# Natural scores of a transformer block: 18 units of 64-query blocks instead of 20 units of 128-query tiles, and another place for them between the expert matmuls

## What is computed

```python
xn = layernorm(x)
q, k, v = split(xn @ w_in.T + b_in)                 # 16 heads of 8
scores = einsum('bhqd,bhkd->bhqk', q / sqrt(8), k) + causal_bias
out = (softmax(scores) @ v).reshape(...) @ w_out.T + b_out
combine = top-2 of softmax(xn @ gate_w.T), normalised, * 2.5
g = silu(xn @ w_gate[e]) * (xn @ w_up[e])           # each expert
y = sum_e combine[e] * (g @ w_down[e]) + shared(xn)
return x + nan_to_zero(out) + y
```

## Time and profile before

| what | value |
|---|---|
| median of 3 runs | 585.33 us (584.45 to 585.44) |
| the profiled execution | 584.21 us |
| its span, first to last instruction | 582.5 us |
| PE, DVE busy | 91%, 81% of the span |
| ACT, POOL busy | 59%, 55% |
| natural scores, maxima on DVE (L1248) | 195.1 us in 224 instructions |
| score matmuls (L561), mask matmuls (L552) | 61.7 and 42.4 us, overlapping |

### The profile page before, as it was taken

How to read it: one execution, slowest core, us unless ns; L and a number is a source line. 1 busy time by engine, 2 the same in 40 slices (tenths; PEclk the granted TensorE clock), 3 DMA queues, 4 the chain that set the end, 5 groups by cost and what they waited for, 6 DMA issues and landing times.

```text
span 582.5 us, 13217 instructions
## 1 busy us (share of the span) xinstructions
PE 531.7 (91%) x4568; PEld 296.5 (51%) x4568; DVE 469.3 (81%) x836; ACT 342.1 (59%) x463; POOL 322.1 (55%) x345
## 2 busy tenths in 40 slices
PE   2779899989999999999999999999999999999985
PEld 1345533656336762476426663366625664366622
DVE  5989788898868978699768988689787988579704
ACT  5422497354973369534893459634794348744593
POOL 2036644675346845478354864478454782558652
PEclk9889999998999999999999999999999999999999
DMA  8994037600376006820168003750069103580001
GB/s 266 270 218 106 11 109 187 160 2 9 110 201 162 2 11 181 226 62 0 63 190 225 0 9 127 210 132 0 9 181 253 35 0 100 173 210 0 11 1 36
DMA packets 45917, 62.03 MB, mean 106 GB/s; under 512 B 4832, under 2 KB 30016, under 8 KB 45888
## 3 DMA queue, kind: packets, MB, share of 16 engines
q1 hardware_dynamic: 43180, 58.40, 36.7%
q10 hardware_dynamic: 2708, 3.24, 1.8%
HBM read 45.24 MB, written 15.34 MB: 104 GB/s over the span
## 4 chain that ended last, share of the span: by engine, by line
PE 58%; ACT 10%; DVE 8%; issue 7%; POOL 4%; POOLq 0%; DVEq 0%; ACTq 0%
PE banks L667 9%; ACT probs L928 8%; PE banks L526 7%; PE banks L561 6%; PE banks L542 6%; PE banks L528 6%; PE banks L527 6%; PE banks L640 6%; DVE neg_max L1248 3%; PE banks L543 3%; PE banks L544 3%; POOL hid_lo L1018 2%; POOL probs L1038 1%; POOL probs L1010 1%; PE banks L552 1%
## 5 line engine op out<-in xcount | busy, mean ns | idle before, releaser
L1248 DVE TENSOR_REDUCE neg_max<-banks 128x2 f32<-128x1024 f32 (+3 forms) x224 | 195.1, 915 | 19.7 <-PE banks L552 18.8
L1010 POOL TENSOR_TENSOR probs<-probs,cb 128x512 f32<-128x512 f32 x88 | 112.9, 1283 | 89.7 <-ACT probs L865 89.7
L928 ACT ACTIVATE probs<-banks 128x1024 f32<-128x1024 f32 x160 | 155.4, 1031 | 11.4 <-PE banks L640 9.0
L1038 POOL TENSOR_SCALAR_AFFINE_SELECT probs<-probs 128x512 f32<-128x512 f32 x128 | 91.4, 736 | 122.2 <-ACT probs L928 122.2
L865 ACT ACTIVATE probs<-banks 128x512 f32<-128x512 f32 (+1 forms) x112 | 66.8, 597 | 139.6 <-PE banks L528 138.8
L1018 POOL TENSOR_TENSOR hid_lo<-probs,hid_hi 128x512 fp32r<-128x512 f32 x85 | 109.3, 1286 | 39.0 <-ACT hid_hi L872 38.9
L526 PE MATMUL banks<-x_hi,w_hi 128*128 128x512 f32 (+1 forms) x224 | 95.4, 426 | 6.1 <-DVE probs L1223 5.3
L667 PE MATMUL banks<-probs,v_op 128*32 128x512 f32 (+3 forms) x1024 | 95.2, 444 | 3.7 <-POOL probs L1038 3.5
L1223 DVE TENSOR_TENSOR probs<-probs,banks 128x512 f32<-128x512 f32 (+1 forms) x112 | 76.0, 680 | 23.5 <-POOL probs L1010 17.2
L528 PE MATMUL banks<-x_hi,w_lo 128*128 128x512 f32 (+1 forms) x224 | 89.5, 399 | 0.0
L527 PE MATMUL banks<-x_lo,w_hi 128*128 128x512 f32 (+1 forms) x224 | 89.1, 398 | 0.0
(11 more groups left out here) (136 smaller groups left out, 557.1 us busy)
## 6 DMA issues: line engine op xcount, KB each, us to landing
cb<-c_dram SPq DMA_DIRECT2D x31, 256.0 KB, 4.2
q_op<-q_dram SPq DMA_DIRECT2D x15, 512.0 KB, 7.1
k_op<-k_dram SPq DMA_DIRECT2D x15, 512.0 KB, 8.3
cb<-c_dram SPq DMA_DIRECT2D x16, 224.0 KB, 4.5
q_dram<-q_parts SPq DMA_DIRECT2D x8, 384.0 KB, 2.6
k_dram<-k_parts SPq DMA_DIRECT2D x8, 384.0 KB, 2.6
cb<-c_dram SPq DMA_DIRECT2D x16, 192.0 KB, 4.4
cb<-c_dram SPq DMA_DIRECT2D x15, 160.0 KB, 4.4
```

The lines of the kernel that those rows point to most:

```text
L928: nc.scalar.activation(probs[:, g % 2, 2 * u:2 * u + 2, :], ring[:, at:at + 2, :], ACT.Exp).then_inc(exp_done, 1)
L1010: nc.gpsimd.tensor_tensor(sg[k % 3][:, :], sg[k % 3][:, :], cb[:, tiles_of(b)[k], :], ALU.mult).then_inc(weighted, 1)
L1038: return nc.gpsimd.affine_select(out=view, in_=view, compare_op=ALU.is_ge, fill=0.0, base=0, pattern=[[0, 4], [1, P]], channel_multiplier=-1)
L1248: return nc.vector.tensor_reduce(out, in_, AX.X, ALU.max, negate=True)
```

## The change

The c of a unit becomes another pair of heads, and queries are taken in blocks of 64 (jq = 0 to 7) that see 64 (jq + 1) keys. A group of four heads then fills 4 units of its own: 512 keys, 448 + 64, 384 + 128 and 320 + 192; the block of 256 keys of two groups shares a ninth. This gives 18 units a batch. Mask matmuls are 64 wide for each block, in all four quarters. The table of maxima is indexed by 8 blocks and 4 groups instead of 4 tiles and 8 pairs, so there are 8 transposes with 64 output partitions, and the copy is 64 partitions x 1024. The places: `PAIRS_AT` ends one tile earlier; in later batches, from tile 4 (`APART`) on, a tile with two units has one in front of gate/up and one behind it, on PE and on DVE. In batch 0 tile 10 has no unit; the split comes after the hidden values of tile 9 and the normalising of the next tokens in tile 12.

```diff
-NAT_PAIRS = 5
+JQ = S // HALF
+OWN_UNITS = 4
+TWO_QUADS = 2 * OWN_UNITS + 1
+NAT_ALL = GROUPS // 2 * TWO_QUADS
...
-UNITS_FIRST = [3 * int(4 <= k <= 9) + 2 * int(k == 10) for k in range(NT + 2)]
+UNITS_FIRST = [3 * int(4 <= k <= 9) for k in range(NT + 2)]
-PAIRS_AT = [int(k in (0, 10)) + 2 * int(1 <= k <= 9) for k in range(NT + 2)]
+PAIRS_AT = [int(k in (0, 9)) + 2 * int(1 <= k <= 8) for k in range(NT + 2)]
 ONE_SLOT = 7
+APART = 4
+def blocks_of(n):
+    two, v = divmod(n, TWO_QUADS)
+    if v == 2 * OWN_UNITS:
+        return [(2 * two, 3, 0), (2 * two + 1, 3, S // 2)]
+    g, long = 2 * two + v // OWN_UNITS, JQ - 1 - v % OWN_UNITS
+    return [(g, long, 0)] + [(g, JQ - 2 - long, HALF * (long + 1))] * int(long < JQ - 1)
...
-                blocks = bank[HALF * c:HALF * (c + 1), a, :].rearrange("p (k n) -> p k n", n=stride)
-                return pe.matmul(blocks[:, at // stride:at // stride + nblk, cols], ident_half[own, :],
-                                 mask_half[own, 0:P - HALF * c].unsqueeze(1).to_broadcast([HALF, nblk, P - HALF * c]),
+                diagonal = bank[rows, a, S - n * width:S].rearrange("p (k n) -> p k n", n=width)[:, :, width - HALF:]
+                return pe.matmul(diagonal, ident_half[own, :],
+                                 mask_half[own, :].unsqueeze(1).to_broadcast([HALF, n, HALF]),
...
-                pe.matmul(bank[rows, a, at:at + n], q_op[own, h // 2, qt * P + HALF * c:qt * P + HALF * (c + 1)],
-                          k_op[own, h // 2, 0:n], start=first, stop=False,
+                n = HALF * (jq + 1)
+                pe.matmul(bank[rows, a, at:at + n], q_op[own, 2 * g + c, HALF * jq:HALF * (jq + 1)],
+                          k_op[own, 2 * g + c, 0:n], start=first, stop=False,
...
-                rows = bank_m[:, 0:S // 2].bitcast(BF16)
-                for q in range(QT):
+                rows = bank_m[0:HALF, :].bitcast(BF16).rearrange("p (c n) -> p c n", c=2)
+                for q in range(JQ):
...
                 for k in range(NT + 2):
+                    front_unit = int(k >= APART and PAIRS_AT[k] == 2)
+                    if front_unit:
+                        pair(b, i, n)
+                        n += 1
                     if 2 <= k < NT:
                         gate_up(b, k)
...
-                    for _ in range(PAIRS_AT[k] - ahead - late):
+                    for _ in range(PAIRS_AT[k] - ahead - late - front_unit):
...
-                    if units and n == NAT_ALL:
+                    if k >= 1 and n == NAT_ALL and UNITS_FIRST[k - 1] and not units:
                         split_maxima(0)
+                    if k == NT - 2:
                         normalise(1)
```

More of the change, by code:

```diff
@@ L175, in block_kernel @@
         after = 2 * FT + NT * E
-        mask_f = early[:, after:after + P]
-        ident_f = early[:, after + P:after + P + HALF]
+        mask_f = early[:, after:after + HALF]
+        ident_f = early[:, after + HALF:after + 2 * HALF]
         hid = [probs[:, 0, n, :] for n in (4, 6, 2)]
@@ L571, in scores @@
                     pe.wait_ge(ops_first, OP_LOADS * 16)
-                elif i is None and n == NAT_PAIRS:
+                elif i is None and n == OWN_UNITS:
                     pe.wait_ge(ops_loaded[0], OP_LOADS * 16)
@@ L590, in scores @@
                 apart(pe, pe_passed)
[L591 to L597, removed]
+                for m, (g, jq, at) in enumerate(blocks):
                     for c in range(2):
                         for a in range(2):
-                            head_scores(bank, a, c, 4 * g + j + a, qt, at, m == 0)
+                            head_scores(bank, a, c, g, jq, at, m == 0)
                 for c in range(2):
                     for a in range(2):
-                        mm = mask_scores(bank, a, c, *masks)
+                        mm = mask_scores(bank, a, c, blocks)
                 mm.then_inc(nat_ready, 1)
@@ L719, in pair @@
             def pair(b, i, n):
-                scores(b, i, n // NAT_PAIRS, n % NAT_PAIRS)
+                scores(b, i, n)
             def first_experts_and_maxima():
@@ L1240, in low_hidden, with maxima @@
                                         ).then_inc(hid_lo_done, 1)
-            def maxima(b, g, v, one_slot):
-                n = NAT_PAIRS * g + v
+            def maxima(b, n, one_slot):
                 dve.wait_ge(nat_ready, NAT_ALL * b + n + 1)
@@ L1248, in neg @@
                     return nc.vector.tensor_reduce(out, in_, AX.X, ALU.max, negate=True)
[L1250 to L1254, removed]
-                else:
-                    last = neg(neg_max[:, 1, :, 2 * g:2 * g + 2, 0], bank[:, :, :].rearrange("p a (k n) -> p a k n", k=2))
+                blocks = blocks_of(n)
+                if n % TWO_QUADS == 2 * OWN_UNITS:
+                    (g, jq, _), _ = blocks
+                    last = neg(neg_max[:, jq, :, g:g + 2, 0], bank[:, :, :].rearrange("p a (k n) -> p a k n", k=2))
+                else:
+                    for g, jq, at in blocks:
+                        last = neg(neg_max[:, jq, :, g, 0], bank[:, :, at:at + HALF * (jq + 1)])
                 last.then_inc(nat_max, 1)
@@ L1355, in pair @@
             def pair(b, i, n):
-                maxima(b, n // NAT_PAIRS, n % NAT_PAIRS, 0 if i is None else ONE_SLOT)
+                maxima(b, n, 0 if i is None else ONE_SLOT)
             def first_experts_and_maxima():
@@ L1405, in experts_and_maxima @@
                         normalise_o(i, 1)
-                    for m in range(PAIRS_AT[k]):
+                    for m in range(PAIRS_AT[k] - front_unit):
                         if k == 1 and m == 1:
```

33 lines of the change are left out of this document (16 added, 17 removed).

## The result

The changed kernel takes **590.5 us** (median of 5 runs, 589.09 to 591.75) against 585.39 us before on the same chip (5 runs, 584.45 to 585.48): a ratio of 1.0091, 95% interval 1.0072 to 1.0109. It is slower, by 0.7 to 1.1%. The forecast was 588.8 us in a range of 581 to 592.

What follows compares the result with a forecast made beforehand. PE was taken to set the pace in later batches, DVE in the first. Seven later batches at +0.89 us gave +6.2, the first -2.7, so +3.5 on 585.33: 588.8 us, range 581 to 592.

Steps and rivals of the forecast that it cites:

- faster rivals: Whole kernel: DVE really sets the pace, 576.6 us, chance 0.14; or changes of matmul size are cheap, 583.2 us, chance 0.13.
- absorbed wait: Later batches: unit 7's wait vanishes because PE later waits for POOL anyway, 585.2 us, no measurable change; chance 0.11.
- worse case: Longer ScalarE copy, 64-column matmuls and two-piece maxima all reach PE: 7 x 0.5 us more, 592 us; chance 0.07.
- PE sets the pace in tiles 4 to 8: Later batches: PE is the limit, DVE stays hidden by little; tiles 5 to 8 take about 3.23 us instead of 3.0.
- 0.31 us more for a unit on either side: Tiles 5 to 8, later batches: one unit each side of gate/up costs PE 0.31 us more than two behind.
- estimate of 0.11 us from the drain: Rival's price per tile: two more drains of 128 cycles at 2.4 GHz cost PE 0.11 us; chance 0.13.
- Unit 7's wait: Tile 4, later batches: the front unit waits for DVE's bias add to free its bank, +0.51 us, bounds 0.3 to 0.8.
- All front units together: Later batch: +1.24 us for front units in tiles 5 to 8 plus +0.51 us for unit 7 in tile 4.
- The 18 units: Later batch: -0.33 us for one unit fewer in tile 9, -0.53 us for shorter masks of fourteen units.
- the cover I named: Tile 12: eight transposes take some 0.25 us more on PE, hidden by its wait for POOL's low part, so 0.
- PE waits for nothing of it now: Later batches: DVE's work is two units less (-2.27 us), plus 0.28 for two-piece maxima, but PE gains nothing.
- The first batch: Batch 0: -0.81 us to gate/up of tile 10 and -2.22 to that of tile 12, sum -2.7 us.

Runs made afterwards that it cites:

- e1: Changed kernel with its 18 units but no unit in front of gate/up in later batches: 577.22 us, ratio 0.9888.
- e4: Kernel before, 20 units of 128 queries, with one unit in front of gate/up from tile 4 in later batches: 598.68 us, ratio 1.0245.
- e2: Changed kernel with a unit in front of gate/up in tile 4 only (unit 7): 581.02 us, ratio 0.994.
- e7: Changed kernel with the first batch's split of the maxima and normalising together right behind the last unit: 592.8 us, ratio 1.0149.
- e8: Kernel before run again without any edit, for its profile alone: 582.11 us, span 580.4 us.
- e3: Changed kernel with units in front of gate/up in tiles 5 to 8 but not in tile 4: 588.31 us, ratio 1.0084.
- e6: e5 with the first batch's normalising one tile earlier, behind the hidden values of tile 10: 575.94 us, ratio 0.9856.
- e5: e1 with the last units spread, one each in tiles 8, 9 and 10: 574.93 us, ratio 0.9853.

## Why the prediction was right, and which terms were off

The sign, the place and the cause came out: 590.5 us lies in the range and in the forecast's own (586.5 to 591). The faster rivals and the absorbed wait fell to e1 to e4, as far as the later batches go; the worse case (592 us) lies close to what was measured, but of its parts the copy on ScalarE made PE wait in no later batch, and only the short matmuls cost something (below). Point by point:

- **PE sets the pace in tiles 4 to 8: right.** Tiles of 3.27 us instead of 3.0, DVE with small gaps (0.17 us at 265.21).
- **0.31 us more for a unit on either side: right.** The absolute prices were each 7 to 17% too high (0.64, 0.49 and 0.82 against 0.57, 0.46 and 0.70), as the masks became shorter, but their difference is 0.33. The tiles give (13.07 - 11.92) / 4 = 0.29, with 11.92 for the same four tiles of e1. The estimate of 0.11 us from the drain in the Trainium skill (TensorE: Matmul & The Clock Gate, the step DRAIN) is a third of it. The rule in the Trainium skill (TensorEngine Tiling (Array Packing), Key Properties) is that a change of tiling mode drains TensorE. The traces agree in that each change of size costs time; by which step inside the engine no run shows.
- **Unit 7's wait: right in kind, 0.51 forecast, 0.69 measured alone (e2).** 0.1 of the difference is the signal, which took 0.15 us instead of 0.05, as all the waiting scores of the kernel before do; the rest is that unit 7 could have followed unit 6 after 0.26 us, not 0.33.
- **All front units together:** 1.24 + 0.51 = 1.75 forecast, 1.94 measured (period of the changed kernel less e1's).
- **The 18 units:** -0.33 - 0.53 = -0.86 forecast, -0.72 measured (e1 less before). By stretches of a later batch (means of five), e1 less before: -0.08 ahead of tile 4; -0.25 in tiles 4 to 7 (264.25 - 252.09 = 12.16 us before, 11.92 in e1) and +0.03 in tile 8, so that ten units gained 0.21 where 0.38 had been forecast for their masks; -0.35 in tile 9; 0 in tiles 10 and 11; +0.12 in tile 12, the transposes (0.13 in the rows above, forecast 0: their change of size was missed, and the cover I named, POOL's low part, was no longer the last to come after tile 10 had lost its unit and PE had waited in tile 11); and **-0.20 behind gate/up of tile 13**, which no term of the forecast has. There PE had waited for DVE's low part, which ended at 279.78:

```profile
279.51 0.40 PE L528 MATMUL banks<-x_hi,w_lo 128*96 128x512 f32 x1
279.84 0.50 PE L542 MATMUL banks<-hid_hi,wd_hi 128*128 128x512 f32 x1
```

  The next matmul follows after another 0.34. In e1 the low part is early and both distances are 0.23. So the forecast's "PE waits for nothing of it now" (of DVE) was not quite so, and this helped by luck: without this gain the 18 units would have been 0.34 off instead of 0.14.
- So a later batch is +1.22 instead of +0.89: **mis-sized terms**, 0.19 for the front units and 0.14 for the 18 units, the second a balance of the parts above.
- **Batch 1 was taken for a batch like the others** and isn't: +0.6 (73.10 against 72.49 us, both with the second dip of the clock), or +0.5 at full clock (72.39 in e7 against 71.87 in e8). DVE's work is on the path there: in the changed kernel PE waits 2.02 us for its hidden values at gate/up of tile 10 (133.27). At full clock e1 and e2 take 70.90 and e3 72.39, as e7: the front units of tiles 5 to 8 cost 1.5, the wait of unit 7 nothing, and the 18 units gain 1.0.
- **The first batch: -2.7 forecast, -1.5 measured at the k projection** (71.77 against 73.25 us), the largest miss. The parts forecast came: from gate/up of tile 6 to that of tile 10 it is 0.78 us less (forecast 0.81), and to tile 12 another 2.10 less (2.22). What failed is the step that ended the sum at tile 12. Behind it the normalising, "behind the hidden values of tile 11", took 2.46 us instead of 1.18, and PE waited 0.53 for it; with the transposes 0.7 was given back. Another 0.7 was lost ahead of it all, at the late operands.
- **Total of the profiles:** -1.5 for batch 0, +0.6 for batch 1, five periods at 1.22, and 1.4 for the last stretch with the end: +6.6, as the spans have it. The medians differ by 5.1 us; the profiled execution of the kernel before was 1.2 us under its median. With the clock of the first 45 us, which differs between executions, that is the order of what single executions can tell.

## What to carry to other kernels

When PE sets the pace, price a move of small tiled matmuls by how many times the array changes between tile sizes, not by the matmuls: two units back to back cost 0.70 us here, and the same two apart 1.03. Look for every such change: halving the output partitions of the transposes made one too. Interleaving them more finely can pay only where PE waits for the consumer; in these tiles it did not, and the same rewriting without it is 1.1% faster than before, or 1.5% with one unit more under the GpSimd-bound tiles. If a moved instruction takes over a bank, look for who still reads it, and follow moved work past the place where the old wait ended, up to the next engine that needs it.

## What had not been expected of the hardware

- **VectorE's tensor_scalar beside GpSimd.** The four normalising instructions (128x128 float32, SBUF to SBUF) take 0.34 us each where GpSimd is idle (337 to 340 ns in e7). Beside GpSimd's tensor_tensor they take up to 1.33. DVE, tile xn, e6 and e7 (min/median/max in ns):

```profile
L1131 DVE TENSOR_SCALAR xn<-x_sb,ln x4: 334/1236/1327, 67.4 to 70.9; 128x128 f32<-128x128 f32 x4
```

```profile
L1131 DVE TENSOR_SCALAR xn<-x_sb,ln x4: 337/338/340, 63.5 to 64.3; 128x128 f32<-128x128 f32 x4
```

A GpSimd instruction takes 1.28 us at the time, so each seems to wait for one of them to end. The Trainium skill says in SBUF — State Buffer, SBUF: two separate sides, that a VectorE instruction in a two-port mode and GpSimd take an exclusive lock on shared ports for a whole instruction. The trace agrees, if these four run in such a mode, which no row shows, and it is the rule that the step on the first batch lacked. Maxima and hidden values, which read PSUM, keep their 0.68 and 1.2 us beside GpSimd.
- **TensorE's clock at the first units.** The dip between 34 and 39 us, seen in most profiles and absent in e8, e3 and e5, is worth 1.4 us, more than some of the effects studied here. A stretch that repeats within 0.05 us from batch to batch tells them; the time of the kernel alone wouldn't.
